# Pairing the Gelus of two expert tiles in a fused Mamba and mixture-of-experts layer on one core

## The reference, cut to what matters

```python
def mamba(x):                                  # 16 states per channel
    x_ssm, x_gate = split(x @ W_in + b_in)
    x_conv = silu(causal_conv4(x_ssm) + conv_b)
    B, C = split(x_conv @ W_bc + b_bc)
    dt = softplus(x_conv @ W_dt + b_dt)
    h[t] = h[t-1] * exp(dt[t] * A) + dt[t] * x_conv[t] * B[t]    # for each state
    y[t] = sum_over_states(h[t] * C[t]) + D * x_conv[t]
    return layernorm((y * silu(x_gate)) @ W_out + b_out + x) * g + b

def experts(x):                                # 8 experts, 2 of them per token
    h = gelu(layernorm(x @ w1[e] + b1[e]) * g1[e] + be1[e])      # 512 wide
    y = h @ w2[e] + b2[e]
    return layernorm(sum_of_two(weight * y) + x) * g + b
```

## Time and profile before

| what | value |
|---|---|
| time, median of 3 runs | 1838.35 us (1836.94 to 1839.93) |
| the profiled execution's own time | 1839.68 us |
| its span, first to last instruction | 1837.7 us |
| busy in the span: PE, DVE, ACT, POOL | 86%, 84%, 79%, 53% |
| mean granted TensorE clock | 0.951 of full speed |
| main loop | about 234 to 1606 us |
| expert tiles alone, and their last stores | about 1606 to 1690 us |

### The profile page before, as it was taken

How to read it: one execution, slowest core, us unless ns; L and a number is a source line. 1 busy time by engine, 2 the same in 40 slices (tenths; PEclk the granted TensorE clock), 3 DMA queues, 4 the chain that set the end, 5 groups by cost and what they waited for, 6 DMA issues and landing times.

```text
span 1837.7 us, 28368 instructions
## 1 busy us (share of the span) xinstructions
PE 1580.6 (86%) x6978; PEld 967.1 (53%) x6978; DVE 1545.9 (84%) x2529; ACT 1458.0 (79%) x2552; POOL 968.3 (53%) x563
## 2 busy tenths in 40 slices
PE   5988389898889888998989898889898998975899
PEld 4555145555556555555555555555555655542344
DVE  4767489999999998989998989999998989811997
ACT  3545379898988989898988889898989898944676
POOL 2767756565555556556655565565556555612000
PEclk9777789999999999999999999999999999988899
DMA  7999743433433333334343333333333333323984
GB/s 236 346 290 350 256 112 83 106 97 83 110 82 93 96 93 85 105 85 107 83 108 91 87 97 91 98 83 100 89 94 85 105 85 108 82 39 75 276 270 148
DMA packets 182857, 234.69 MB, mean 128 GB/s; under 512 B 45865, under 2 KB 148524, under 8 KB 182719
## 3 DMA queue, kind: packets, MB, share of 16 engines
q1 hardware_dynamic: 141234, 171.83, 30.3%
q0 software_dynamic: 26160, 36.06, 10.5%
q10 hardware_dynamic: 15328, 25.20, 4.1%
HBM read 149.33 MB, written 83.70 MB: 127 GB/s over the span
## 4 chain that ended last, share of the span: by engine, by line
DVE 33%; ACT 25%; PE 21%; issue 13%; DMA 4%; ACTq 3%; POOL 1%; SPq 0%; another core or an unknown queue 0%; DVEq 0%; POOLq 0%
DVE area L1276 7%; DVE area L1289 5%; ACT area L660 4%; DVE area L1306 4%; DVE area L1285 3%; PE psX L975 3%; ACT psD L654 3%; PE psT L1023 3%; DVE more L1338 3%; ACT h_T L694 3%; ACT L702 3%; ACT L699 3%; DMA area<-L_attn_x 2%; DVE more L1335 2%; DVE h_norm L1319 2%
## 5 line engine op out<-in xcount | busy, mean ns | idle before, releaser
L539 POOL TENSOR_TENSOR area<-area,more 128x1024 f32<-128x1024 f32 x258 | 604.4, 2360 | 553.2 <-DVE area L1289 279.2
L1306 DVE TENSOR_TENSOR area<-area,psD 128x1024 f32<-128x1024 f32 x256 | 310.1, 1211 | 0.2 <-PE psD L988 0.2
L965 PE MATMUL psH<-w_sb,ffn_xT 128*128 x544 | 265.8, 612 | 5.8 <-ACT ffn_xT L670 5.7
L975 PE MATMUL psX<-w_sb,h_T 128*128 x1088 | 267.0, 389 | 0.8 <-ACT y_out L676 0.8
L516 POOL DMA_INDIRECT expert_d<-y_out,meta x139 | 220.7, 1588 | 83.3 <-ACT y_out L676 56.9
L996 PE MATMUL psY<-ident,area 128*128 128x128 f32 x2048 | 250.7, 276 | 0.0
L975 PEld LDWEIGHTS psX<-w_sb,h_T 128*128 128x128 f32 x1088 | 205.8, 193 | 60.6 <-issue 32.4
L660 ACT ACTIVATE area<-area,A_sb 128x512 f32<-128x512 f32 x258 | 171.5, 712 | 74.2 <-DVE area L1289 40.8
L996 PEld LDWEIGHTS psY<-ident,area 128*128 128x128 f32 x2048 | 222.2, 141 | 13.4
L694 ACT ACTIVATE h_T<-psT,be_T,g_T 128x128 f32<-128x128 f32 x540 | 202.2, 459 | 4.7 <-PE psT L955 4.7
L654 ACT ACTIVATE psD<-area,A_sb 128x512 f32<-128x512 f32 x258 | 177.9, 690 | 31.6 <-DVE area L1276 12.3
(11 more groups left out here) (186 smaller groups left out, 2515.4 us busy)
## 6 DMA issues: line engine op xcount, KB each, us to landing
more<-B_rows_d SPq DMA_DIRECT2D x130, 512.0 KB, 4.0
xin<-sorted_x SPq DMA_DIRECT2D x137, 128.0 KB, 2.1
more<-ssm_d SPq DMA_DIRECT2D x18, 512.0 KB, 3.7
area<-xnT_d SPq DMA_DIRECT2D x17, 512.0 KB, 3.5
mamba_d<-mo_stage SPq DMA_DIRECT2D x17, 512.0 KB, 2.9
area<-L_attn_x SPq DMA_DIRECT2D x8, 1024.0 KB, 6.9
xnT_d<-w_sb ACTq DMA_DIRECT2D x16, 512.0 KB, 6.6
expert_d<-area ACTq DMA_DIRECT2D x8, 1024.0 KB, 8.9
```

Source lines behind the costliest of these rows:

```text
L539: pool.tensor_tensor(inflow[:, k], dtx, B_rep[par][:, k].rearrange("p (a t) -> p a t", a=1).to_broadcast([P, KD, CHUNK]), ALU.mult).then_i ...
L965: nc.tensor.matmul(psH[:, :], ffn_xT[:, k, :], w1_sb[:, bass.ds(e, 1), k, :].rearrange("p o h -> p (o h)"), start=(k == 0), stop=False)
L975: nc.tensor.matmul(psX[:, DIM:2 * DIM], h_T[:, buf, k, :], w2_sb[:, bass.ds(e, 1), k, :].rearrange("p o d -> p (o d)"), start=(k == 0), st ...
L1306: V.tensor_tensor(h, h, C_rep[k].rearrange("p (a t) -> p a t", a=1) .to_broadcast([P, KD, CHUNK]), ALU.mult).then_inc(S[f"hC{k}_done"], 1)
```

## The change

The Gelus of tiles u-1 and u stand together in the turns with even pr, between one load of the Gelu set and one of the Exp set; turns with odd pr have no Gelu. Both Silus stand at pr 1. On PE, transpose_h stands behind up; in odd turns it is the last thing, behind a wait for ACT's copy of this turn's projection; in even turns the projection is last, behind the Gelus. transpose_sum stands behind transpose_h at pr 0. Down projections come one turn later, as do their scaled copies and scatters, so there are two buffers for the normalised hidden layer and three for the Gelus' results. copy_y stands in front of the table load. The expert numbers are read beside their use instead of at the turn's start. On SP, store_mamba(16) stands behind the last tile loads. Dummy operations that filled the pipeline at its start are gone. The diff, cut to its core and with its indents shortened:

```diff
-LAG = 2
+LAG = 3
...
-GATE_TURN = 2
...
+        h_T2 = scan_area.take(KH, P)
+        h_norm2 = scan_area.take(HIDDEN)
...
+        h_norms = [h_norm[:, :], h_norm2]
+        h_Ts = [h_T[:, 0], h_T[:, 1], h_T2]
...
-store_mamba(CHUNKS)
...
+store_mamba(CHUNKS)
...
-sp.wait_ge(S["y_stored"], 16 * (FFN_TURNS + LAG + 2))
+sp.wait_ge(S["y_stored"], 16 * FFN_TURNS)
...
-def scatter_y(slot, buf):
-    pool.indirect_dma_start(out=expert_d, out_offset=bass.IndirectOffsetOnAxis(ap=meta_tok[:, slot, :], axis=0),
-                            in_=y_out[:, buf, :], in_offset=None, compute_op=ALU.add).then_inc(S["y_stored"], 16)
...
-def y_at_hand(u):
-    pool.wait_ge(S["y_copied"], u + 1 + 1)
-    pool.wait_ge(S["y_stored"], 16 * (u + 2))
+def y_at_hand(t):
+    pool.wait_ge(S["y_copied"], t + 1)
+    if t > 0:
+        pool.wait_ge(S["y_stored"], 16 * t)
...
+def scatter_y(t):
+    pool.indirect_dma_start(out=expert_d, out_offset=bass.IndirectOffsetOnAxis(ap=meta_tok[:, t % RING, :], axis=0),
+                            in_=y_out[:, t % 2, :], in_offset=None, compute_op=ALU.add).then_inc(S["y_stored"], 16)
...
-scatter_y((-2 - LAG) % RING, 0)
...
-            y_at_hand(u - 1)
+            if u > LAG:
+                y_at_hand(u - 1 - LAG)
...
-            scatter_y((pr - 1 - LAG) % RING, (pr - 1) % 2)
-for u in range(MAMBA_TURNS - 1, FFN_TURNS + LAG):
-    y_at_hand(u)
-    scatter_y((u - LAG) % RING, u % 2)
...
-pool.wait_ge(S["y_stored"], 16 * (FFN_TURNS + LAG + 2))
+            if u > LAG:
+                scatter_y(u - 1 - LAG)
+for t in range(MAMBA_TURNS - 1 - LAG, FFN_TURNS):
+    y_at_hand(t)
+    scatter_y(t)
...
+pool.wait_ge(S["y_stored"], 16 * FFN_TURNS)
...
-act.sem_inc(S["gelu_done"], 1)
-act.sem_inc(S["y_copied"], 1)
...
 def copy_xT(t):
...
-    if isinstance(t, int) and t == 0:
-        act.wait_ge(S["y_ready"], 1)
-    else:
-        act.wait_ge(S["y_ready"], t)
+    if t > 0:
...
+    if t > LAG:
+        act.wait_ge(S["y_ready"], t - LAG)
...
-def copy_y(u, slot, buf, e):
-    act.wait_ge(S["y_ready"], u + 1)
-    act.wait_ge(S["y_stored"], u * 16 + 16)
-    nc.scalar.activation(y_out[:, buf, :], psX[:, DIM:2 * DIM], ACT.Copy, scale=meta[:, slot, bass.ds(e, 1)]
+def copy_y(t):
+    act.wait_ge(S["y_ready"], t + 1)
+    if t >= 2:
+        act.wait_ge(S["y_stored"], 16 * (t - 1))
+    nc.scalar.activation(y_out[:, t % 2, :], psX[:, DIM:2 * DIM], ACT.Copy, scale=meta[:, t % RING, bass.ds(expert(t), 1)]
...
-def gelu(u, buf, e):
...
-    act.wait_ge(S["hT_done"], u + 1 + 1)
+def gelu(u):
...
+    e = expert(u)
+    act.wait_ge(S["hT_done"], u + 1)
+    if u >= 3:
+        act.wait_ge(S["y_ready"], u - 2)
...
-        a = nc.scalar.activation(h_T[:, buf, k, :], psT[:, k * P:(k + 1) * P], ACT.Gelu,
+        a = nc.scalar.activation(h_Ts[u % 3][:, k, :], psT[:, k * P:(k + 1) * P], ACT.Gelu,
...
-            e, e_y = expert(u), expert(u - LAG)
...
+            if u >= LAG:
+                copy_y(u - LAG)
...
-            with_gelu()
-            copy_y(u, (pr - LAG) % RING, pr % 2, e_y)
-            gelu(u, pr % 2, e)
+            if pr % 2 == 0:
+                with_gelu()
+                if u > 0:
+                    gelu(u - 1)
+                gelu(u)
+                with_exp()
...
+                gate_silu_of(c, half)
...
-            if pr == GATE_TURN:
-                gate_silu_of(c, half)
-            with_exp()
+                with_exp()
...
-    e, e_y = expert(u), expert(u - LAG)
...
+    copy_y(u - LAG)
...
-    copy_y(u, (u - LAG) % RING, u % 2, e_y)
-    gelu(u, u % 2, e)
+    if u == MAMBA_TURNS:
+        gelu(u - 1)
+    gelu(u)
...
-for u in range(FFN_TURNS, FFN_TURNS + LAG):
-    copy_y(u, (u - LAG) % RING, u % 2, expert(u - LAG))
+for t in range(FFN_TURNS - LAG, FFN_TURNS):
+    copy_y(t)
...
-for name, ahead in (("tr_ready", 1), ("sum_done", 2), ("hT_done", 1)):
+for name, ahead in (("tr_ready", 1), ("sum_done", 2)):
...
 def transpose_x(t):
...
-    if not (isinstance(t, int) and t == 0):
+    if t > 0:
...
-    if not (isinstance(t, int) and t < 2):
-        pe.wait_ge(S["y_copied"], t - 1 + 1)
+    if t >= LAG + 2:
+        pe.wait_ge(S["y_copied"], t - 1 - LAG)
...
 def transpose_h(u):
...
-    pe.wait_ge(S["norm_done"], u + 1 + 1)
-    pe.wait_ge(S["gelu_done"], u + 1)
+    pe.wait_ge(S["norm_done"], u + 1)
+    if u > 0:
+        pe.wait_ge(S["gelu_done"], u)
...
-        m = nc.tensor.transpose(psT[:, k * P:(k + 1) * P], h_norm[:, k * P:(k + 1) * P], ident[:, :])
+        m = nc.tensor.transpose(psT[:, k * P:(k + 1) * P], h_norms[u % 2][:, k * P:(k + 1) * P], ident[:, :])
...
-def up(t, e):
+def up(t):
+    e = expert(t)
...
-    pe.wait_ge(S["norm_done"], t + 1)
+    if t > 0:
+        pe.wait_ge(S["norm_done"], t)
...
-def down(u, buf, e):
...
-    pe.wait_ge(S["y_copied"], u + 1 + 1 + 1)
-    pe.wait_ge(S["gelu_done"], u + 1 + 1)
+def down(t):
...
+    e = expert(t)
+    if t > 0:
+        pe.wait_ge(S["y_copied"], t)
+    pe.wait_ge(S["gelu_done"], t + 1)
...
-        nc.tensor.matmul(psX[:, DIM:2 * DIM], h_T[:, buf, k, :], w2_sb[:, bass.ds(e, 1), k, :].rearrange("p o d -> p (o d)"),
+        nc.tensor.matmul(psX[:, DIM:2 * DIM], h_Ts[t % 3][:, k, :], w2_sb[:, bass.ds(e, 1), k, :].rearrange("p o d -> p (o d)"),
...
-for k in range(KD):
-    m = nc.tensor.transpose(psX[:, DIM + k * P:DIM + (k + 1) * P], ident[:, :], ident[:, :])
-m.then_inc(S["y_ready"], 1)
...
-up(0, expert(0))
+up(0)
...
-            e_down, e_up = expert(u - 1), expert(u + 1)
-            if pr == 0:
-                wait_taken("gate1", c)
-            elif TASKS[pr - 1] is not None:
-                wait_taken(TASKS[pr - 1], g)
-            transpose_h(u)
-            up(u + 1, e_up)
+            if u == 0:
+                wait_taken("gate1", 0)
+                transpose_h(0)
+            up(u + 1)
...
-            early_C = pr not in (CONV_TURN - 1, CONV_TURN, DT_TAKEN + 1)
-            if early_C:
+            if pr % 2 == 0:
+                if u > 0:
+                    transpose_h(u)
...
-                spread_C1(u + 1, state[1], par)
-            if pr == 0:
-                transpose_sum(c)
+                if pr == 0:
+                    transpose_sum(c)
+                early_C = pr not in (CONV_TURN - 1, DT_TAKEN + 1)
+                if early_C:
+                    spread_C1(u + 1, state[1], par)
+                if u >= 2:
+                    down(u - 2)
+                if not early_C:
+                    spread_C1(u + 1, state[1], par)
+                if pr == 0:
+                    seed(c)
+                add_up(u, pr % 2)
+                if TASKS[pr] is not None:
+                    pe.wait_ge(S["gelu_done"], u + 1)
+                    task(TASKS[pr], g)
...
-                pe.wait_ge(S["gelu_done"], u + 1 + 1)
-            if pr == TASKS.index("out0"):
-                project_out(c, 0, psT[:, :])
-            elif pr == TASKS.index("out1"):
-                project_out(c, 1, psT[:, :])
-            elif TASKS[pr] is not None:
-                task(TASKS[pr], g)
-            if not early_C:
-                transpose_x(u + 2)
-                spread_C1(u + 1, state[1], par)
-            down(u - 1, (pr + 1) % 2, e_down)
-            if pr == 0:
-                seed(c)
-            add_up(u, pr % 2)
-wait_taken("gate1", CHUNKS)
+                early_C = pr != CONV_TURN
+                if early_C:
+                    transpose_x(u + 2)
+                    spread_C1(u + 1, state[1], par)
+                pe.wait_ge(S["gelu_done"], u)
+                if TASKS[pr - 1] is not None:
+                    wait_taken(TASKS[pr - 1], g)
+                if pr == TASKS.index("out0"):
+                    project_out(c, 0, psT[:, :])
+                elif pr == TASKS.index("out1"):
+                    project_out(c, 1, psT[:, :])
+                else:
+                    task(TASKS[pr], g)
+                if not early_C:
+                    transpose_x(u + 2)
+                    spread_C1(u + 1, state[1], par)
+                if u >= 2:
+                    down(u - 2)
+                add_up(u, pr % 2)
+                wait_taken(TASKS[pr], g)
+                transpose_h(u)
...
-    e_down, e_up = expert(u - 1), expert(u + 1)
+    up(u + 1)
...
-    up(u + 1, e_up)
...
-    down(u - 1, (u - 1) % 2, e_down)
-down(FFN_TURNS - 1, (FFN_TURNS - 1) % 2, expert(FFN_TURNS - 1))
+    down(u - 2)
+for t in range(FFN_TURNS - 2, FFN_TURNS):
+    down(t)
...
-for name, ahead in (("logits_taken", 1), ("norm_done", 1), ("scan0_done", 1), ("scan1_done", 1), ("hC0_done", 1), ("hC1_done", 1),
+for name, ahead in (("logits_taken", 1), ("scan0_done", 1), ("scan1_done", 1), ("hC0_done", 1), ("hC1_done", 1),
...
 def hidden_norm(u):
...
-    dve.wait_ge(S["hT_done"], u + 1)
-    V.tensor_scalar(h_norm[:, :], psH[:, :], hmv[:, 0:1], hrs[:, 0:1], ALU.subtract, ALU.mult
+    if u >= 2:
+        dve.wait_ge(S["hT_done"], u - 1)
```

(3 more changed lines are left out.)

## The result

The changed kernel takes **1918.63 us** (median of four runs, 1915.97 to 1919.69), the kernel before on the same chip 1839.14 (1836.94 to 1844.03): ratio 1.0426, 95% interval 1.0402 to 1.045. It is slower, as forecast, but by 79 us instead of 36, and the range ended at 1902. The profiled execution took 1918.38 us, with a span of 1916.6 and a mean granted clock of 0.927 (before: 0.951).

The account below looks back on a forecast made before the run. It took DVE as nearest to full, idle mainly waiting for ACT's root. 1839.7 + 34 (loop, 16 chunks at +2.15) + 2 (tail) = 1876, or 1874 us beside the median; range 1848 to 1902.

Parts of the forecast that it names:

- what the block costs: ACT's work from turn 4's root to turn 5's: a second Gelu group with handover lengthens DVE's wait by 2.3 us.
- a forecast of +2.15: Loop: the turns' terms together make each chunk 2.15 us longer, times 16 +34 us.
- turns 2 and 3: ACT from turn 2 to 3: 2.3 us come in, the gate's Silu with its load, 2.34, leaves: +0.1 us.
- I cost PE at nothing more: PE in the loop: stands of some 2 us in turns 3, 5 and 7, covered by about 9 us spare per chunk.
- Rival C: PE in the loop: its clock falls more often, thirteen more windows at 1.9 us, 25 in all: 1899 us; chance 0.15.
- The -1.5 of turn 6: From turn 5 to 6: ACT loses a Gelu group and two loads, so DVE's wait of 1.48 us goes.
- Turn 7: From turn 6 to 7: 2.3 us more on ACT exceed its 1.42 to spare; +0.75 us taken.
- The gate's +0.5: From turn 0 to 1: transpose_sum behind transpose_h makes the gate's operand late, +0.5 us, bounds nothing and 1.50.
- B: Loop: the loads set the pace and DVE's waits vanish, 1771 us, faster; chance 0.10.
- D: Loop: the second Gelu group costs less, turn 5 +1.2 us and the gate nothing: 1849 us; chance 0.15.
- The tail: Behind the loop: earlier loads -6, five turns +3, last scatters +4.8, later start +0.4; in all +2 us.
- Its signs: Profile after: loads 88 and 71, root waits in turns 3, 5, 7, none in 6, chunk 86.5 to 88 us.

Follow-up runs that it names:

- e1: The changed kernel with ACT's copy_xT ahead of its take of the projection in odd turns; 1885.19 us, ratio 1.0229.
- e2: The changed kernel with eight idle matmuls on PE ahead of up's wait for copy_xT in turns 3, 5 and 7; 1892.54 us, ratio 1.0271.
- e10: e1 with DVE's finish_dt moved from the end of turn 6 to behind scan0_of of turn 7; ratio 1.0211.
- e4: The kernel before with only the gate's Silu moved from turn 2 to turn 1; 1831.55 us, ratio 0.992.
- e5: e1 with POOL's scatter in turn 6 held back until DVE's finish_dt is done; ratio 1.0219.
- e9: e1 with the expert numbers read at the start of each turn again, on ACT and PE; ratio 1.0185.

## Why the prediction was right and wrong

- **Right: what the block costs.** Turns 4 and 5 at +2.3 (e1: +2.36; the root's wait there is 1.12 before and 3.41 in e1), the loads, no root wait in turn 6, the longest in turn 5. e1 gives +2.24 a chunk for a forecast of +2.15; in part by luck, because errors cancel, since its turns 2 and 3 cost 0.48 for 0.1, turn 6 gained 0.67 for 1.5, and the gate and turn 7 cost 0.04 for 1.25.
- **Wrong: "I cost PE at nothing more".** The prediction laid out the stand of some 2 us in turns 3, 5 and 7 rightly (2.38 measured) and covered it with "about 9 us to spare per chunk". That slack is a sum over a chunk; what counts is the time that PE has from its up to the add_up of the same turn before DVE needs it. From the stand in PE's turn 3 that was too little by 0.5 us even at full clock (9.03 for 8.50), and by 2.1 with a fall. Measured: +2.05 a chunk between e1 and the changed kernel, 32 us. The prediction had this as an end, 0.5 per odd turn and 32 us, and did not take it; its range ended at 1902, below even 1874 + 32. That the end was met to the microsecond is luck: it had no clock in it, and 20 of the 32 are the clock's.
- **Rival C was the mechanism, at the wrong size and chance.** It put one fall per chunk at 1.9 us, 25 us in all, and left the price of the stand itself at nothing. There are 1.93 a chunk, of which little more than one is in a place where it costs 1.6 us, and filling the stands gives back 20 us; C's sum was of that size. Its 1.9 us had a weak ground, since the third window of the earlier trace rows, at a clock of 0.96, has nearly the DVE work of the first (79.77 and 79.96). The argument against it, that PE had stood 1 to 2 us and kept its clock, was no argument for stands of 2.4, and in e1 the clock falls behind stands of 1.7 too. The Trainium skill, "TensorE: Matmul & The Clock Gate", Part 1, had the rule that an idle PE is halved; e2 agrees.
- **The -1.5 of turn 6 was -0.95.** The removed wait had kept DVE clear of POOL's multiply, and the add grew from 1.22 to 1.93 to 2.27 us (mean 2.09), so part of the gain was given back at once. How much of it the loop would get back is not shown: e10 took the longer add away and got 0.24 in turns 6 and 7 and nothing in the chunk. The prediction asked what is late next, not what DVE now runs into.
- **Turn 7**: +0.75 forecast, +0.99 measured, but for another reason: in e1, where PE is in time, it is -0.06. The gate's +0.5 (+0.81) likewise came from PE.
- **B** fell as argued: the handover and the second group are in the block. **D** did not come: turn 5's price is whole wherever PE is in time.
- **The tail**, forecast +2, came to +8. The stores: -7.4 for -6. The five turns: +9.3 for +3, the order's own cost and the register read as above, and the clock, which was not in the sum. The last scatter: +5.6 for +4.8. The start of the tail: +0.6 for +0.4. (From the last scatter to the end of the kernel it is 1 us less than before.)
- **Its signs.** The loads came out as named, and turn 6 has no wait for the root. The chunk, 90.07, is above the 86.5 to 88 that it had named. DVE waits for add_up in 26 places, not in most turns, and those few places were enough.

## What to carry to other kernels

Slack of an engine over a stretch covers nothing unless it lies between the late step and the one who waits for it: follow the engine from its new wait to its next deadline within the turn. Where a reordering gives PE new stands (here 2.4 us), look at the granted clock behind each, and cost the work that follows at the lower level if another engine waits for it; the number of falls alone says little (20 in e1, and its loop is within 3 us of the forecast). Here it was enough to let another engine's copy for PE pass ahead of the one that only drains its last result. And when a wait goes, lay the freed engine's next operations beside what the others are doing at that time.

## What the runs showed of the hardware that I had not expected

- Eight useless matmuls in three stands of PE per chunk made the loop 20 us shorter (e2), because up took 1.98 and not 3.1 to 3.6 us behind them.
- The same stand of 2.4 us was followed by a fall of the clock in 8 chunks of 14 and not in the others. What decides between them no run here shows.
- A DVE operation with both operands in SBUF waits for the end of a POOL multiply under way (1.22 becomes 1.93 to 2.27 us, 0.69 becomes 1.41 to 2.16 in e4), and operations with a PSUM operand do not (1.22 and 1.21 beside it in e5). A scatter that POOL issued during such an add took 2.38 instead of 1.58 us.
- With the register reads at another place of the turn the clock fell 9 times and not the 20 of e1 in 14 chunks (e9), with the same work on every engine. By what this comes about I did not settle.
